# Four graph layers on one core: reworked stage ends, late edge cells inside the first head, and a node cell that reads its gates from PSUM

## What is computed

```python
x = _layernorm(x + relu(A_norm @ (x @ W0) + b0))                       # layer 0
Wh = x @ W1                                                            # layer 1, one attention head
att = softmax(where(adj > 0, leaky_relu(Wh @ a1 + (Wh @ a2).T), -9e15))
x = _layernorm(x + relu(att @ Wh))
pos, neg = (adj > 0) @ x, (adj < 0) @ x                                # layer 2
x = _layernorm(x + concat(pos, neg) @ Wn + bn * diag(adj) + (adj @ x) @ We + be * diag(adj))
edge = gru_cell(adj0 @ x, x, edge_weights)                             # layer 3; adj0: adj without its diagonal
sup  = mean over 3 heads k of (softmax_masked(e_k) * adj0) @ (x @ gat_W[k])
node = gru_cell(sup, x, node_weights)
x = _layernorm(x + diag(adj) * edge + diag(adj) * node)
# gru_cell(i, h): r, z = sigmoid(i_r + h_r), sigmoid(i_z + h_z); n = tanh(i_n + r * h_n); (1 - z) * n + z * h
```

## Time and profile before

| | us |
|---|---|
| median of three runs | 1569.28 |
| the profiled execution | 1568.71 |
| its span, from the first to the last instruction of the trace | 1567.0 |
| PE busy | 1378.0 (88%) |
| DVE busy | 939.5 (60%) |
| ACT busy | 537.1 (34%) |
| POOL busy | 171.2 (11%) |
| granted PE clock, mean | 0.942 |

### The profile page before, as it was taken

One profiled execution on the slowest core, in us unless ns is written; L12 is line 12 of the kernel. 1 busy time (PEld: TensorE's weight loads), 2 busy tenths in 40 slices (PEclk: granted clock), 3 DMA queues, 4 the chain that ended last, 5 costly groups with the idle time before them and its releaser, 6 DMA issues.

```text
span 1567.0 us, 12683 instructions
## 1 busy us (share of the span) xinstructions
PE 1378.0 (88%) x4557; PEld 725.9 (46%) x4557; DVE 939.5 (60%) x1388; ACT 537.1 (34%) x419; POOL 171.2 (11%) x196
## 2 busy tenths in 40 slices
PE   3787885579994999998999999799999999999982
PEld 1333333434443444445555455545545454544561
DVE  4888886458876000002025363598778987898587
ACT  3343431447743000000110001355555556455321
POOL 0000000420000000001000000133111321125100
PEclk9999897689997999999899999999999999999996
DMA  9999990000003666665566427588786878688101
GB/s 364 405 405 401 406 381 10 2 1 0 0 0 103 195 193 195 194 183 173 175 207 203 146 81 245 197 302 306 271 299 225 321 284 294 229 319 312 66 1 44
DMA packets 99919, 318.82 MB, mean 203 GB/s; under 512 B 11009, under 2 KB 26240, under 8 KB 86272
## 3 DMA queue, kind: packets, MB, share of 16 engines
q1 hardware_dynamic: 99840, 317.83, 57.9%
HBM read 314.38 MB, written 3.41 MB: 203 GB/s over the span
## 4 chain that ended last, share of the span: by engine, by line
PE 75%; DMA 11%; DVE 8%; issue 2%; POOL 2%; ACT 1%; SPq 1%; DVEq 0%
PE ps L1082 27%; DMA ring<-in_adjB 11%; PE ps L842 10%; PE ps L925 9%; PE ps L889 9%; PE ps L883 5%; PE ps L781 4%; PE ps L987 2%; POOL y L488 2%; PE ps L1003 1%; DVE x L1197 1%; PE ps L906 1%; PE ps L1064 1%; PE ps L907 1%; PE ps L866 1%
## 5 line engine op out<-in xcount | busy, mean ns | idle before, releaser
L1082 PE MATMUL ps<-arena,x 128*128 128x512 f32 (+1 forms) x1092 | 443.3, 564 | 10.4 <-DVE arena L1589 8.8
L1082 PEld LDWEIGHTS ps<-arena,x 128*128 128x128 f32 x1092 | 205.7, 191 | 239.7 <-issue 226.5
L702 ACT ACTIVATE arena<-arena,bench 128x3328 f32<-128x3328 bf16 x78 | 239.6, 3073 | 201.0 <-PE ps L1082 197.3
L781 PE MATMUL ps<-ring,bench 128*128 128x512 f32 (+1 forms) x364 | 174.9, 627 | 43.3 <-DMA ring<-in_adjB 43.3
L1589 DVE TENSOR_TENSOR arena<-arena,ring 128x3328 f32<-128x3328 f32 x52 | 189.3, 3640 | 38.9 <-ACT arena L702 38.9
L889 PE MATMUL ps<-ring,x 128*128 128x512 f32 (+1 forms) x364 | 175.7, 564 | 0.0
L925 PE MATMUL ps<-ring,x 128*128 128x512 f32 (+1 forms) x364 | 157.1, 585 | 3.7 <-DVE x L1197 3.7
L1322 DVE SCALAR_TENSOR_TENSOR bench<-b,cols,ps 128x128 f32<-128x128 f32 x26 | 7.3, 343 | 208.1 <-PE ps L866 208.1
L781 PEld LDWEIGHTS ps<-ring,bench 128*128 128x128 f32 x364 | 72.2, 209 | 125.4 <-issue 83.2
L883 PE MATMUL ps<-arena,shared 128*128 128x512 fp8e4 (+1 forms) x364 | 103.5, 366 | 16.1 <-DVE shared L1317 16.1
L1589 DVE TENSOR_TENSOR arena<-arena 128x3328 f32<-128x3328 f32 x26 | 94.3, 3627 | 19.1 <-ACT arena L702 19.1
(11 more groups left out here) (254 smaller groups left out, 1506.2 us busy)
## 6 DMA issues: line engine op xcount, KB each, us to landing
ring<-in_adjB SPq DMA_DIRECT2D x468, 256.0 KB, 3.6
ring<-in_adjR SPq DMA_DIRECT2D x52, 1664.0 KB, 7.7
arena<-in_adjR SPq DMA_DIRECT2D x26, 1664.0 KB, 7.7
shared<-in_adj SPq DMA_DIRECT2D x7, 1664.0 KB, 14.5
es<-in_adj SPq DMA_DIRECT2D x7, 1664.0 KB, 14.2
xT<-in_adj SPq DMA_DIRECT2D x6, 1664.0 KB, 14.6
ring<-in_adjB SPq DMA_DIRECT2D x78, 128.0 KB, 2.5
y<-in_adj SPq DMA_DIRECT2D x6, 1664.0 KB, 14.4
```

The lines of the kernel that those rows point to most:

```text
L702: A_(E[n % 3], below[n % 3], ACT.Exp, bias=tt_[:, t * HEADS + k:t * HEADS + k + 1], scale=-WIN).then_inc(e_exp, 1)
L781: mm(ps[:, b, 0:w], lhsT=scaled[:, t % 4], rhs=ring[:, n % CHUNKS, 0:w], start=(t == 0), stop=(t == TILES - 1)).then_inc(ring_free, 1)
L1082: last = mm(ps[:, b, 0:w], lhsT=x[:, t], rhs=E[n % 3][:, o_:o_ + w], start=(t == 0), stop=(t == TILES - 1))
```

## The change

What it does, stage by stage:
- **End of layer 0**: DVE's loop is written out, `hb4` gives each parity its own buffer, and the statistics of group g-1 stand between the bias step and the `y` step of group g. PE and ACT keep their hardware loops.
- **Start of layer 1**: POOL writes the last column of `y` first, then the tiles, and PE waits for each tile of `y` alone. ACT makes five blocks of `rp`, each as soon as its own product is done, DVE the other two; tile 0 is cut, exponentiated and weighed in two parts (four blocks, three blocks). Four small DVE steps (`faint_row`) move behind tile 4.
- **End of layer 1**: ACT evicts four blocks of `UT` and DVE three; POOL adds `x` in place of DVE; the statistics lag by two groups.
- **Before layer 2**: `split_x` of two tiles follows their normalization inside `norm(1)`, ahead of the branch.
- **Layer 3**: `MN` and an identity `ident16` are bf16, so `spread_points` multiplies bf16. `gate_products` has three products for each tile in place of four (weights rolled on the host). The last block's first 13 slots lie in the ring's second half, and row tile 1 is loaded into its first half during that block. Edge cells 10, 11 and 12 and the eviction of block 6 move into head 0: their `gru_a` stands between `lower` and `weigh` of the first tiles, their other steps after tiles 3, 5, 9, 11, 15 and 17.
- **Node cell**: the bias is added by a bf16 product of a row of ones with three bf16 parts of the bias (made by ten DVE steps in layer 0, `split_bias`), `gru_a` is gone, tanh and `node_b` read PSUM, POOL makes `x - n`, three sets of buffers, gates in banks 0 to 3 and transposes in banks 5 and 6, and PE waits per block of `es` and not for all of it.

```diff
+        def NG(par):
+            return ps[:, 2 * par:2 * par + 2, :]
+
+        def NU(par):
+            return ps[:, 5 + par, 0:GW]
...
+            if b == NB - 1:
+                return ring_flat[:, NP + t % CHUNKS * GW:NP + t % CHUNKS * GW + w]
+            return ring[:, t % CHUNKS, 0:w]
...
-                ring_load(R3, n, b, t, w)
+                sp.wait_ge(ring_free, CHUNKS + R3 + slot4_free(b, t))
+                sp.dma_start(slot4(b, t, w), d["adjB"][b, t, :, 0:w]).then_inc(ring_in[t % CHUNKS], 16)
+                if b == NB - 1 and t == CHUNKS - 1:
+                    sp.dma_start(rows[1], d["adjR"][1]).then_inc(row_in[1], 16)
...
+            g_.tensor_copy(y[:, :, F - 1:F], fade[:, :, None]).then_inc(xp_done, 1)
             for t in range(TILES):
-                g_.tensor_scalar(y[:, t], x[:, t], fade[:, t:t + 1], None, ALU.mult).then_inc(xp_done, 1)
-            pool.wait_ge(xp_done, TILES)
-            g_.tensor_copy(y[:, :, F - 1:F], fade[:, :, None]).then_inc(xp_done, 1)
+                g_.tensor_scalar(y[:, t, 0:F - 1], x[:, t, 0:F - 1], fade[:, t:t + 1], None, ALU.mult).then_inc(xp_done, 1)
+
+            def layer2(general):
+                if general:
+                    return
+                for k in range(GROUPS):
+                    pool.wait_ge(z_out, 2 + GROUPS + k + 1)
+                    g_.tensor_tensor(y[:, 2 * k:2 * k + 2], hb4[:, 2 * (k % 2):2 * (k % 2) + 2], x[:, 2 * k:2 * k + 2],
+                                     ALU.add).then_inc(y_done, 1)
+            either(pool, layer2, 1)
...
-        MN = sb("MN", [P, TILES, HEADS])
+        MN = sb("MN", [P, TILES, HEADS], BF16)
+        ident16 = gb[:, 1].rearrange("p a f -> p (a f)")[:, 3 * F:3 * F + P // 2].bitcast(BF16)
...
+            for g in range(GROUPS):
+                w = three_spaces[g % 3]
+                pool.wait_ge(n_done, GROUPS + g + 1)
+                g_.tensor_tensor(w.hm, x[:, 2 * g:2 * g + 2], w.n, ALU.subtract).then_inc(hm_done, 1)
...
-            for b, (o_, w) in enumerate(BLOCKS):
-                act.wait_ge(f1_done, NB)
+            for b, (o_, w) in enumerate(BLOCKS[:RP_ACT]):
+                act.wait_ge(f1_done, b + 1)
                 A_(rp[:, o_:o_ + w], ps[:, b, 0:w], ACT.Relu, bias=spans[:, 0:1]).then_inc(rp_done, 1)
...
+                    elif t == 0:
+                        for n, (lo, hi) in enumerate(PARTS):
+                            act.wait_ge(low1_part, n + 1)
+                            A_(EL[0][:, lo:hi], EL[0][:, lo:hi], ACT.Exp, scale=ALPHA - 1).then_inc(exp1_part, 1)
...
-                    A_(UT[:, o_:o_ + w], ps[:, b, 0:w], ACT.Identity, bias=xsb).then_inc(ut1, 1)
-                    if b >= 2:
-                        relu_pair(2 * b - 4)
-                        relu_pair(2 * b - 3)
-                for k in range(2 * NB - 4, GROUPS):
+                    if b % 2 == 0:
+                        A_(UT[:, o_:o_ + w], ps[:, b, 0:w], ACT.Identity, bias=xsb).then_inc(ut1, 1)
+                        if b >= 4:
+                            relu_pair(b // 2 - 2)
...
-                            edge_cell(GROUPS - 1)
+                            u3_copy(NB - 1)
+                        if k == 0:
+                            for n in range(3):
+                                if t == LATE_AT[n] - 1:
+                                    gru_tanh(LATE + n, late_spaces[n])
+                                if t == LATE_AT[n] + 1:
+                                    gru_cand(LATE + n, late_spaces[n])
...
+            def node_tanh(g):
+                act.wait_ge(g3_done, GROUPS + g + 1)
+                if g >= 3:
+                    act.wait_ge(gru_done, GROUPS + g - 2)
+                A_(three_spaces[g % 3].pre, NG(g % 2)[:, :, F:G3], ACT.Tanh, scale=0.5).then_inc(th_done, 1)
...
-                pe.wait_ge(xp_done, TILES + 1)
                 for t in range(TILES):
-                    pe.wait_ge(q1, t + 1)
+                    pe.wait_ge(xp_done, t + 2)
+                    if t:
+                        pe.wait_ge(q1, t)
                     for b, (o_, w) in enumerate(BLOCKS):
+                        if t == 0 and b in (0, FIRST):
+                            pe.wait_ge(q1_part, 1 if b == 0 else 2)
...
-                    mm(gt[:, G3:4 * F], lhsT=ht, rhs=gru[:, 2 * e + 1, 2 * F:], start=True, stop=True)
-                    mm(gt[:, 2 * F:G3], lhsT=ut, rhs=gru[:, 2 * e, 2 * F:], start=True, stop=True)
-                    mm(gt[:, 0:2 * F], lhsT=ut, rhs=gru[:, 2 * e, 0:2 * F], start=True, stop=False)
-                    last = mm(gt[:, 0:2 * F], lhsT=ht, rhs=gru[:, 2 * e + 1, 0:2 * F], start=False, stop=True)
+                    mm(gt[:, G3:4 * F], lhsT=ut, rhs=gru[:, 0, 2 * F:], start=True, stop=True)
+                    mm(gt[:, 0:G3], lhsT=ht, rhs=gru[:, 1], start=True, stop=False)
+                    last = mm(gt[:, F:G3], lhsT=ut, rhs=gru[:, 0, 0:2 * F], start=False, stop=True)
...
-                    last = mm(ps[:, bank, tt * P:(tt + 1) * P], lhsT=MN[:, t, k:k + 1].to_broadcast([P, P]), rhs=ident[:],
+                    last = mm(ps[:, bank, tt * P:(tt + 1) * P], lhsT=MN[:, t, k:k + 1].to_broadcast([P, P]), rhs=ident16,
...
-            pe.wait_ge(es_done, 1)
             def node_gates(g):
                 pe.wait_ge(u7_out, g + 1)
-                gate_products(GROUPS + g, 1, ub[:, g % 2], 0, g * GW)
+                if g < 2:
+
+                    pe.wait_ge(zh_out, (HEADS - 1) * NB + 3 + 2 * g)
+                else:
+                    pe.wait_ge(cand_done, GROUPS + g - 1)
+                for tt in range(2):
+                    gt = NG(g % 2)[:, tt]
+                    ut = ub[:, g % 2, tt * P:(tt + 1) * P]
+                    ht = xT[:, g * GW + tt * P:g * GW + (tt + 1) * P]
+                    mm(gt[:, 0:4 * F], lhsT=ones16, rhs=bias_parts, start=True, stop=False)
+                    mm(gt[:, F:4 * F], lhsT=ut, rhs=gru[:, 2], start=False, stop=False)
+                    last = mm(gt[:, 0:G3], lhsT=ht, rhs=gru[:, 3], start=False, stop=True)
+                last.then_inc(g3_done, 1)
...
+                pe.wait_ge(zh_out, (HEADS - 1) * NB + g // 2 + 1)
...
+            def split_bias():
+                for n in range(3):
+                    step(v.tensor_copy(part_, node_bias))
+                    if n < 2:
+                        step(v.tensor_tensor(node_bias, node_bias, part_, ALU.subtract))
+                    mask = ident[0:3, n:n + 1]
+                    if n == 0:
+                        step(v.tensor_scalar(taken, part_, mask, None, ALU.mult))
+                    else:
+                        step(v.scalar_tensor_tensor(taken if n == 1 else bias_parts, part_, mask, taken, ALU.mult, ALU.add))
+                step(v.tensor_copy(ones16, ones[0:3, :]))
+                step(v.tensor_copy(ident16, ident[:]))
...
+                if t == 4:
+                    split_bias()
...
+                    if layer == 1 and t % 2:
+                        split_x(t // 2)
+
+
+            def split_x(c):
+                cut = slice(2 * c, 2 * c + 2)
...
+            def finish0(g):
                 ve.wait_ge(z_done, 2 + g + 1)
                 for tt in range(2):
-                    op = v.scalar_tensor_tensor(hb[:, tt], Z0(par)[:, tt], column(D, g * 2 + tt), b0[:], ALU.mult, ALU.add)
+                    op = v.scalar_tensor_tensor(hb4[:, g % 2 * 2 + tt], Z0(g % 2)[:, tt], D[:, 2 * g + tt:2 * g + tt + 1], b0[:], ALU.mult, ALU.add)
                 op.then_inc(z_out, 1)
+                if g:
+                    statistics0(g - 1)
                 ve.wait_ge(z_out, 2 + g + 1)
-                v.scalar_tensor_tensor(y[:, bass.ds(g * 2, 2)], hb[:], 0.0, x[:, bass.ds(g * 2, 2)], ALU.max,
-                                       ALU.add).then_inc(y_done, 1)
-                statistics(0, g)
-            groups(ve, finish0)
+                v.scalar_tensor_tensor(y[:, 2 * g:2 * g + 2], hb4[:, g % 2 * 2:g % 2 * 2 + 2], 0.0, x[:, 2 * g:2 * g + 2],
+                                       ALU.max, ALU.add).then_inc(y_done, 1)
...
+                for b, (o_, w) in enumerate(BLOCKS):
+                    if b >= RP_ACT:
+                        ve.wait_ge(f1_done, b + 1)
+                        v.tensor_scalar(rp[:, o_:o_ + w], ps[:, b, 0:w], spans[:, 0:1], 0.0, ALU.add, ALU.max).then_inc(rp_rest, 1)
...
+                ve.wait_ge(rp_done, FIRST)
+                cut_part(0)
+                scores_rest()
+                ve.wait_ge(rp_done, RP_ACT)
+                ve.wait_ge(rp_rest, NB - RP_ACT)
+                cut_part(1)
                 cut_scores(1)
-                for t in range(TILES):
+                weigh_part(0)
+                weigh_part(1)
+                for t in range(1, TILES):
                     if t + 2 < TILES:
                         cut_scores(t + 2)
                     weigh(t)
+                    if t == 4:
+                        faint_row()
 
...
+                    if k <= 2:
```

(41 more changed lines are left out.)

228 lines of the change are left out of this document (137 added, 91 removed).

## The result

The changed kernel takes 1519.07 us in the median of four runs (1516.25 to 1519.82), the kernel before on the same chip 1568.22: a ratio of 0.9682 (95% interval 0.9671 to 0.9694). The direction was right. The size was not: 49 us, where the sum gave 73.5, and the time lies above the range, which ended at 1511.

The account below looks back on a forecast made before the run. TensorE, with 75% of the chain of work that ended last, was taken as the bound. Gains of 6.8 + 16.0 + 2.8 + 9.5 + 11.0 + 10.0 + 17.4 = 73.5 us gave a median of 1495.8; range 1486 to 1511.

Parts of the forecast that it names:

- End of layer 0: Groups at layer 0's end cost 1.40 us in place of 2.08, with statistics in the gap and two buffers; gain 6.8 us.
- The rival of the hardware loops on ACT and TensorE: End of layer 0: these loops set the pace, so 6 us come back, 1501.8; chance 0.12.
- Start of layer 1: TensorE starts layer 1 near 307.2 in place of 323.79; gain 16.6 us, 16.0 after 0.6 lost in the loop.
- End of layer 1, x16: POOL's add paces pairs at 0.78, gain 2.8 us; before layer 2 DVE's branch falls where nobody waits, gain 9.5 us.
- Point products: Layer 3: 78 products on TensorE's path, each 0.14 us cheaper in bf16; gain 11.0 us.
- Edge cells and first head tiles: Seam into the heads: tile 0 starts right behind the gates and tile 1 10.3 us earlier; gain taken as 10.0 us.
- TensorE's own branch cost 0.76 of its weight loads elsewhere: Ahead of head tile 0: TensorE's branch costs 0.76 us, so tile 0 starts at 1006.4.
- the rival: Behind the last gates: the branch stops TensorE, tile 0 starts 2.7 us later at the low clock, 1500.9; chance 0.14.
- When row tile 1 is in the ring too: Ahead of the heads: row tile 1 is loaded by about 1003.6, when DVE has weighed tile 0.
- Node cell: TensorE becomes the bound at 3.25 us a group in place of 4.4 on DVE; gain 17.4 us.
- the bias row, 2 x 512 columns in one pass of four, 0.43: Node cell: the bias products of a group cost TensorE 0.43 us of its 3.25.
- The rival with POOL: Node cell: DVE holds up POOL's `x - n`, a group rises to about 4.0 us, 1505.6; chance 0.13.

Follow-up runs that it names:

- experiment 4: Changed kernel with the node cell's `x - n` computed on DVE in place of POOL; 1519.88 us, 0.9689.
- experiment 9: Changed kernel with the point products back in fp32 in place of bf16; 1524.11 us, 0.9719.
- experiment 5: Changed kernel with SP holding back the loads of row tiles 2 and 3 until TensorE has used head tile 0; 1520.11 us, 0.9685.
- experiment 1: Changed kernel with TensorE's heads code for this input, and the node cell's products, placed straight behind the branch; 1508.45 us, 0.9625.
- experiment 2: Changed kernel with row tile 1 loaded after the last slot of block 6 in place of ahead of slot 13; 1512.83 us, 0.9645.
- experiment 3: Changed kernel with the node cell's bias product left out; 1507.85 us, 0.9625.
- experiment 8: Changed kernel with TensorE heads and DVE layer 1 code behind their branches, row tile 1 loaded later, bias in a row of ones, no bias product; 1493.21 us, 0.9525.

## Why the prediction was right or wrong

**End of layer 0: right mechanism, too small.** DVE runs at 1.24 a group, not 1.40: with the statistics in the gap the steps overlap so closely that a group takes less than the sum of the row lengths, 1.51, which I had called the upper end. The rival of the hardware loops on ACT and TensorE is out.

**Start of layer 1: right, 1.9 too large.** TensorE started at 299.43 with the chain that I had described. The branch of DVE cost 4.61, not the 3.47 of the earlier trace rows, and the cuts and weighings 8.2 from 291.23 to TensorE's start, where I had 7.4. POOL's tiles of `y` took up to 7.34 us, longer than the 5.79 of the earlier trace rows, and it still was never the last for TensorE: seven tiles were ready before DVE's first cut, where I had counted on five.

```profile
L544 POOL TENSOR_SCALAR y<-x,cols x26: 606/612/7344, 286.9 to 327.9; 128x127 f32<-128x127 f32 x26
```

The Trainium skill (GPSIMD Engine Reference, Specifications) says that POOL shares its SBUF interfaces with VectorE; this row and experiment 4 agree, and experiment 4 adds that VectorE's own steps get longer as well.

**End of layer 1, x16: right**, 0.6 too small together. The pace of a pair is 0.76 to 0.83 by POOL's adds, and nothing stands between the normalization and the cast: the cast starts at 466.12, TensorE at 466.93.

**Point products: right, 1.0 too small in the price** (0.155 saved for each, for which I took 0.14). They are 12.1 us on TensorE, yet going back to fp32 cost only 5.0 to 5.8 (experiment 9), since the stalls of the seam changed with it.

**Edge cells and first head tiles: wrong, 14.4 us.** Three steps of the prediction failed.
- "TensorE's own branch cost 0.76 of its weight loads elsewhere." This row stands where TensorE's queue had work: in the trace of before the two packets of that branch pass between 802 and 803 and between 806 and 807, while the products of block 1 run without a gap from 797.98 to 807.59. I took it against the 3.47 of DVE's row. On the path it cost 7.4, twice what even the rival had (2.7 us of delay and a low clock for tile 0). The rival named the mechanism and had it too cheap: it left out that a fetch goes through the DMA engines, where two row loads were running, and that a second one follows. The Trainium skill (Runtime: NRT & Kernel Launch, Instruction fetch mechanics) says that an engine fetches its code in blocks of 16 KiB through a DMA queue of its own and that a taken branch outside the window forces a fetch. The packets of 0.02 MB at 976 and 981 agree. That the wait grows with the other loads, 1.90 against 5.26, is shown by experiment 5. The trace of before had the warning at this very branch: its DMA view has a packet of 16 KB on queue 8 between 1008 and 1009, inside the 7.52 us of idle time that DVE's weighing ended, and another between 1013 and 1014. The branch was free there only because DVE was later, and the change took DVE out of the way. The row from 1008 to 1009:

```profile
q8 instruction: 1, 0.02, 5.8%
```

- "When row tile 1 is in the ring too." I counted the load as one of SP's issues that came for free. It takes 9.9 us to land, in the middle of block 6, and the 13 small slots stand behind it. My text weighed only whether the first slots of block 6 were late.
- The low clock: tile 0, 5.75 us at full clock (experiment 1), took 9.07 us of TensorE's time, at a granted clock of 0.63, behind TensorE's rests. So a stall cost about one and a half times its length: by the traces 10.3 for 7.4 in experiment 1 and 4.9 for 3.28 in experiment 2.

**Node cell: right that TensorE becomes the bound, 8.0 too large.** The failed step is "the bias row, 2 x 512 columns in one pass of four, 0.43". It is 0.9 to 1.0 (experiment 3), which in 13 groups is some 7 of the 8.0. The fp32 columns and the transposes at 2.58 + 0.22 were right to 0.03: without bias a group takes 2.82. The bound from DVE, 2.75, was low too (2.96), but hidden. The rival with POOL (period 4.0) fits the time better than my 3.25 and is wrong all the same: experiment 4 takes POOL out and nothing moves.

**What I had at nothing: the low clock in stretches of tiny products.** The 26 products of two columns (52 instructions) take 9.66 us at a granted clock of 0.58 after the change, 8.41 at 0.67 before, and 7.04 at 0.82 in the profile of experiment 3, whose code is the same up to there. Rows of before, and of experiment 3:

```profile
280.64:289.05 8.41, 8.41 (x55) 8.41 (x53) 0.00 (x0) 2.38 (x6) 0.00 (x0) 0.67 0.00 0
```

```profile
269.87:276.91 7.04, 7.04 (x55) 7.04 (x54) 0.00 (x0) 2.30 (x6) 0.00 (x0) 0.82 0.00 0
```

So here it is no fixed price of the change (experiments 5 and 8 have 7.00 and 6.90 too, the other seven 9.35 to 9.97). The two such stretches of layer 3, of six and of three columns, are another case: they take 9.78 to 10.16 and 9.25 to 9.62 in all eleven profiles from the changed kernel on, and 8.83 and 6.84 in the one of before, so there the change may have a part. With the start of layer 2, 1.1 slower than before, the stages in which these lie came out 4.2 us below the forecast (1.5, 1.1 and 1.6 in the table). Why the clock falls where it does was not tried and stays open.

The sum of all this: 14.4 + 8.0 + 1.9 + 1.3 for layer 1's loop + 4.2 in the stages with the low clock is 29.8; less 2.3 + 2.1 + 0.6 + 0.7 that came out better it is 24.1, the miss. With both stalls of the seam and DVE's branch out of the way and the bias products paired the kernel runs at 1497.5, near the 1495.8 of the prediction: that was about the time of a kernel without the stalls that it had left out. How near it comes is partly luck: the forecast had DVE's branch in it, and a bias product that costs half of what it does. The low ends of the gains add up to 46.2, so "near 1520" for all of them together should read 1523.
